# Moving the bias, v's copies and two statistics steps off GpSimd in a fused attention and FP4 feed-forward layer

## The reference

```python
xn = (x - mean) / sqrt(var + eps)
q, k, v = rope(xn @ Wqa @ Wqb), rope(k of xn @ Wkva @ Wkvb), v of the same
attn = softmax(causal(q @ k.T * scale)) @ v @ Wout + bout
h = silu(fp4(xn) @ fp4(w_gate).T) * (fp4(xn) @ fp4(w_up).T)
out = x + attn + fp4(h) @ fp4(w_down).T
```

## Time and profile before

| | |
|---|---|
| median of 3 runs | 807.89 us (806.34 to 809.37) |
| the profiled execution, its time and its span | 808.11 us, 806.0 us |
| PE busy in the span | 718.5 us (89%), 6354 instructions |
| DVE | 641.2 us (80%) |
| POOL | 612.4 us (76%) |
| ACT | 535.1 us (66%) |
| mean granted TensorE clock | 0.98 |

### The profile page before, as it was taken

How to read it: one execution, slowest core, us unless ns; L and a number is a source line. 1 busy time by engine, 2 the same in 40 slices (tenths; PEclk the granted TensorE clock), 3 DMA queues, 4 the chain that set the end, 5 groups by cost and what they waited for, 6 DMA issues and landing times.

```text
span 806.0 us, 18255 instructions
## 1 busy us (share of the span) xinstructions
PE 718.5 (89%) x6354; PEld 444.2 (55%) x6445; DVE 641.2 (80%) x1378; ACT 535.1 (66%) x1154; POOL 612.4 (76%) x708
## 2 busy tenths in 40 slices
PE   2366889999999999999999999999999999999773
PEld 1233555665656565656656565656566565656243
DVE  5569788989888988889898889888898988788110
ACT  2212677777686867777777868677777777575850
POOL 4534597878799797978787897979787888756560
PEclk9998899999999999999999999999999999999995
DMA  4423233243343334343434333343324333330111
GB/s 111 114 67 96 63 93 95 89 116 96 103 111 103 88 114 106 112 100 91 115 97 107 102 110 87 113 106 116 96 90 118 94 95 111 88 92 29 56 55 28
DMA packets 85589, 76.04 MB, mean 94 GB/s; under 512 B 28946, under 2 KB 67314, under 8 KB 85498
## 3 DMA queue, kind: packets, MB, share of 16 engines
q1 hardware_dynamic: 85498, 74.87, 34.3%
HBM read 40.73 MB, written 27.53 MB: 85 GB/s over the span
## 4 chain that ended last, share of the span: by engine, by line
PE 35%; POOL 32%; ACT 14%; issue 6%; DVE 6%; DMA 3%; SPq 2%; another core or an unknown queue 1%; POOLq 0%; DVEq 0%; ACTq 0%
POOL P L535 9%; PE pv_ps L1111 8%; PE exp_ps L1090 6%; POOL h L545 5%; ACT P L912 5%; PE max_ps L1075 5%; POOL h L548 5%; POOL h L551 4%; PE misc_ps L1135 3%; PE misc_ps L1143 3%; DVE neg_max L718 3%; PE max_ps L1076 3%; PE misc_ps L1160 3%; ACT h_mag L1019 3%; POOL q_split L626 2%
## 5 line engine op out<-in xcount | busy, mean ns | idle before, releaser
L718 DVE TENSOR_REDUCE neg_max<-max_ps 128x1 f32<-128x512 f32 (+3 forms) x768 | 429.1, 591 | 88.3 <-PE max_ps L1076 86.6
L912 ACT ACTIVATE P<-exp_ps 128x512 f32<-128x512 f32 x512 | 294.9, 599 | 167.0 <-remote 100.4
L1075 PE MATMUL max_ps<-K,Q 128*128 128x384 bf16 (+2 forms) x768 | 199.2, 278 | 23.4 <-DMA Kd<-K 11.2
L1090 PE MATMUL exp_ps<-Q,K 128*128 128x128 bf16 (+3 forms) x933 | 209.9, 293 | 10.8 <-ACT P L912 6.7
L1076 PE MATMUL max_ps<-Kd,Q 128*128 128x128 bf16 x1024 | 191.4, 221 | 1.4 <-DVE neg_max L718 1.3
L535 POOL TENSOR_SCALAR_AFFINE_SELECT P<-P 128x512 f32<-128x512 f32 x256 | 161.9, 667 | 26.8 <-ACT P L915 26.8
L1111 PE MATMUL pv_ps<-P,V 128*32 128x512 f32 (+3 forms) x2048 | 163.9, 438 | 1.9 <-POOL P L535 0.8
L1075 PEld LDWEIGHTS max_ps<-K,Q 128*128 128x128 bf16 x768 | 75.9, 100 | 92.1 <-DVE neg_max L718 47.1
L1076 PEld LDWEIGHTS max_ps<-Kd,Q 128*128 128x128 bf16 x1024 | 98.6, 100 | 45.6 <-issue 23.2
L1090 PEld LDWEIGHTS exp_ps<-Q,K 128*128 128x128 bf16 x1024 | 79.6, 98 | 48.6 <-ACT P L912 27.0
L566 POOL TENSOR_TENSOR h<-gate_sb,up_half 128x352 f32<-128x352 f32 x64 | 59.7, 932 | 56.8 <-DVE gate_sb L731 56.6
(11 more groups left out here) (109 smaller groups left out, 977.5 us busy)
## 6 DMA issues: line engine op xcount, KB each, us to landing
Q<-q_scr SPq DMA_DIRECT2D x64, 224.0 KB
o_scr<-oT SPq DMA_DIRECT2D x32, 256.0 KB, 2.5
q_scr<-q_split SPq DMA_DIRECT2D x16, 384.0 KB, 2.6
Kd<-K SPq DMA_DIRECT2D x64, 96.0 KB
x_in<-x SPq DMA_DIRECT2D x16, 256.0 KB, 4.6
q_scr<-q_split SPq DMA_DIRECT2D x16, 256.0 KB, 2.9
x_res<-x SPq DMA_DIRECT2D x16, 256.0 KB, 5.5
o_raw<-o_scr SPq DMA_DIRECT2D x32, 128.0 KB
```

The source lines that it names most:

```text
L718: nc.vector.tensor_reduce(neg_max[:, pr // 4, heads[0]:heads[0] + len(heads), pr % 4, i], max_ps[r % 3][:, 0:len(heads) * n].rearrange("p ...
L912: nc.scalar.activation(P[g % 2][:, hh + r % 2, col:col + 512], ps[:, :], ACT.Exp, scale=SCALE).then_inc(exp_done, 1)
L1075: nc.tensor.matmul(ps[:, col:col + d], Qt, Kt[:, half, g, 0:d], start=True, stop=True)
L1090: last = nc.tensor.matmul(exp_ps[n % 2][:, col:col + width], K[par][:, half, pr // 2, kb * 128:(kb + 1) * 128], Q[par][:, pr, kb * 128:S], ...
```

## The change

Four things are done. The bias bout becomes a 97th row of the third piece of wdT, beside a row of ones in hqT, so that PE's output matmul adds it; x_bias goes, DVE adds x_res itself, and SP loads x_res for batch T-1 in iteration T, behind the last read of "out1" of the iteration before. v_stage goes: DVE writes v from PSUM into V with two copies, and there are three V tiles in place of two. Of `statistics`, POOL keeps rstd alone; var_eps is made by DVE between two reductions of slot 3, and shift by DVE ahead of the first reduction of slot 5, behind a wait for rstd (neg_mean is folded into it). At the start DVE sets the row of ones, and POOL clears a third V tile.

```diff
+    def third(self, off):
+        return (self.t0 + off) % 3
-        V = [sb(f"V{i}", [128, NT, KVH, 32]) for i in range(2)]
+        V = [sb(f"V{i}", [128, NT, KVH, 32]) for i in range(3)]
...
 # SP
-                (bout_sb[:, :], bout.partition_broadcast(128)),
+                (wdT[FC[2][1]:FC[2][1] + 1, 2, :], bout.unsqueeze(0)),
...
-                if T.has(0):
-                    T.wait(sp, x_bias_done, 1, 0, 0)
-                    sp.dma_start(x_res[:, :, :], x[T.batch(0)]...).then_inc(x_res_loaded, 16)
+                if T.has(-1):
+                    T.prev().misc_wait(sp, misc_read, "out1")
+                    sp.dma_start(x_res[:, :, :], x[T.batch(-1)]...).then_inc(x_res_loaded, 16)
...
 # GpSimd
-            def statistics(T):
+            def deviation(T):
                 if not T.has(3):
                     return
-                T.wait(pool, mv_done, NT, 3, NT)
-                nc.gpsimd.tensor_scalar(var_eps[:, :], bn_mv[:, :, 1], EPS, None, ALU.add).then_inc(var_done, 1)
-                nc.gpsimd.tensor_scalar(neg_mean[:, :], bn_mv[:, :, 0], -1.0, None, ALU.mult).then_inc(var_done, 1)
-                T.wait(pool, var_done, 2, 3, 2)
+                T.wait(pool, var_done, 1, 3, 1)
                 nc.gpsimd.tensor_tensor(rstd[:, :], var_eps[:, :], half_neg[:, :], ALU.pow).then_inc(rstd_done, 1)
-                T.wait(pool, rstd_done, 2, 3, 1)
-                nc.gpsimd.tensor_tensor(shift[:, :], neg_mean[:, :], rstd[:, :], ALU.mult).then_inc(rstd_done, 1)
...
-                if T.has(1):
-                    T.prev().misc_wait(pool, misc_read, "v")
-                    if T.has(-1):
-                        T.wait(pool, pv_done, KVH, -1, KVH)
-                    for s in range(2):
-                        nc.gpsimd.tensor_copy(V[T.par(1)]..., v_stage...).then_inc(v_ready, 1)
...
-                if T.has(0):
-                    T.wait(pool, x_res_loaded, 16, 0, 16)
-                    T.misc_wait(pool, misc_read, "out1")
-                    nc.gpsimd.tensor_tensor(x_bias[:, :, :], x_res[:, :, :], bout_sb...).then_inc(x_bias_done, 1)
...
 # VectorE
-                                        x_bias[:, c, :], ALU.add).then_inc(misc_read[0], 1)
+                                        x_res[:, c, :], ALU.add).then_inc(misc_read[0], 1)
...
-                reduces(3, 4, 5)
+                reduces(3, 4)
+                if T.has(3):
+                    T.wait(dve, mv_done, NT, 3, NT)
+                    T.wait(dve, rstd_done, 2, 2, 1)
+                    nc.vector.tensor_scalar(var_eps[:, :], bn_mv[:, :, 1], EPS, None, ALU.add).then_inc(var_done, 1)
+                reduces(3, 5)
                 if T.has(2):
                     T.misc_wait(dve, misc_filled, "v")
-                    T.wait(dve, v_ready, 2, 1, 2)
-                    nc.vector.tensor_copy(v_stage[:, :, :], misc_ps[1][:, 0:128]...).then_inc(misc_read[1], 1)
+                    if T.has(-1):
+                        T.wait(dve, pv_done, KVH, -1, KVH)
+                    for odd in range(2):
+                        nc.vector.tensor_copy(V[T.third(2)][:, :, odd::2, D * odd:D * odd + D],
+                                              misc_ps[1][:, 0:128]...[:, :, odd::2, :]
+                                              ).then_inc(v_ready if odd == 0 else misc_read[1], 1)
...
+                if T.has(3):
+                    T.wait(dve, rstd_done, 2, 3, 1)
+                    nc.vector.scalar_tensor_tensor(shift[:, :], bn_mv[:, :, 0], -1.0, rstd[:, :],
+                                                   ALU.mult, ALU.mult).then_inc(rstd_done, 1)
                 reduces(5, 0)
                 normalize(T)
...
+            nc.vector.memset(hqT[FC[2][1]:FC[2][1] + 1, 2, :], 1.0).then_inc(ones_row, 1)
...
 # TensorE
-                        for k, (_, cn) in enumerate(FC):
+                        for k, cn in enumerate((FC[0][1], FC[1][1], FC[2][1] + 1)):
                             last = nc.tensor.matmul(ps[:, tok[n]], hqT[0:cn, k, tok[c]], wdT[0:cn, k, :], ...)
```

More of the change, by code:

```diff
@@ L151, in build @@
         wout_sb = sb("wout_sb", [E, E])
-        bout_sb = sb("bout_sb", [128, E])
         cosq_sb = sb("cosq_sb", [128, S])
@@ L171, in build @@
         rstd = sb("rstd", [128, NT])
-        neg_mean = sb("neg_mean", [128, NT])
         shift = sb("shift", [128, NT])
@@ L185, in build @@
         k_split = sb("k_split", [128, 3, 128], BF16)
-        v_stage = sb("v_stage", [128, NT, KVH * D])
         Q = [sb(f"Q{i}", [128, NPAIR, S], BF16) for i in range(2)]
@@ L203, in build @@
         x_res = sb("x_res", [128, NT, E])
-        x_bias = sb("x_bias", [128, NT, E])
         y = sb("y", [128, NT, E])
@@ L237, in build @@
         const_dma = sem("const_dma")
+        ones_row = sem("ones_row")
         factors_in = sem("factors_in")
@@ L280, in build @@
         x_res_loaded = sem("x_res_loaded")
-        x_bias_done = sem("x_bias_done")
         stored = sem("stored")
@@ L459, in iteration @@
             def iteration(T):
-                if T.has(0):
-                    T.wait(sp, x_bias_done, 1, 0, 0)
-                    sp.dma_start(x_res[:, :, :], x[T.batch(0)].rearrange("(c p) e -> p c e", p=128)).then_inc(x_res_loaded, 16)
+                if T.has(-1):
+                    T.prev().misc_wait(sp, misc_read, "out1")
+                    sp.dma_start(x_res[:, :, :], x[T.batch(-1)].rearrange("(c p) e -> p c e", p=128)).then_inc(x_res_loaded, 16)
                 scatter_sums(T, -1, 1)
@@ L515, in _ @@
             nc.gpsimd.memset(half_neg[:, :], -0.5).then_inc(consts_set, 1)
-            for i in range(2):
+            for i in range(3):
                 nc.gpsimd.memset(V[i][:, :, :, :], 0.0).then_inc(pool_const, 1)
@@ L520, in _ @@
             nc.gpsimd.memset(m_split[:, :, 64:128], 0.0).then_inc(pool_const, 1)
-            pool.wait_ge(pool_const, 5)
-            for i in range(2):
+            pool.wait_ge(pool_const, 6)
+            for i in range(3):
                 nc.gpsimd.memset(V[i][:, :, 0::2, 2 * D:2 * D + 1], 1.0).then_inc(pool_const, 1)
@@ L603, in iteration @@
                     causal(T, 0, 0)
-                if T.has(1):
-                    T.prev().misc_wait(pool, misc_read, "v")
-                    if T.has(-1):
-                        T.wait(pool, pv_done, KVH, -1, KVH)
-                    for s in range(2):
-                        nc.gpsimd.tensor_copy(V[T.par(1)][:, :, s::2, D * s:D * s + D],
-                                              v_stage[:, :, :].rearrange("p c (g d) -> p c g d", g=KVH)[:, :, s::2, :]).then_inc(v_ready, 1)
                 if T.has(2):
@@ L633, in iteration @@
                     nc.gpsimd.tensor_tensor(k_split[:, 2, :], k_rest[:, :], k_split[:, 1, :], ALU.subtract).then_inc(k_pool, 1)
-                statistics(T)
+                deviation(T)
                 split_rest(T, 1, 0)
@@ L644, in iteration @@
                     quantize(T, 0, 3, *hs)
-                if T.has(0):
-                    T.wait(pool, x_res_loaded, 16, 0, 16)
-                    T.misc_wait(pool, misc_read, "out1")
-                    nc.gpsimd.tensor_tensor(x_bias[:, :, :], x_res[:, :, :],
-                                            bout_sb[:, :].unsqueeze(1).to_broadcast([128, NT, E]), ALU.add).then_inc(x_bias_done, 1)
                 if T.has(3):
@@ L765, in output @@
                 if n == 0:
-                    T.wait(dve, x_bias_done, 1, -1, 1)
+                    T.wait(dve, x_res_loaded, 16, -1, 16)
                     T.wait(dve, stored, 32, -1, 0)
@@ L831, in iteration @@
                     T.wait(dve, x_loaded, 16, 3, 16)
-                    T.wait(dve, var_done, 2, 2, 2)
                     for c in range(NT):
@@ L843, in iteration @@
                         nc.vector.bn_aggr(bn_mv[:, c, :], bn_raw[:, c, :]).then_inc(mv_done, 1)
-                reduces(3, 4, 5)
+                reduces(3, 4)
[4 more added lines that the diff above has]
+                reduces(3, 5)
                 if T.has(2):
                     T.misc_wait(dve, misc_filled, "v")
-                    T.wait(dve, v_ready, 2, 1, 2)
-                    nc.vector.tensor_copy(v_stage[:, :, :], misc_ps[1][:, 0:128].rearrange("p (c n) -> p c n", c=NT)).then_inc(misc_read[1], 1)
+                    if T.has(-1):
+                        T.wait(dve, pv_done, KVH, -1, KVH)
+                    for odd in range(2):
+                        nc.vector.tensor_copy(V[T.third(2)][:, :, odd::2, D * odd:D * odd + D],
+                                              misc_ps[1][:, 0:128].rearrange("p (c g d) -> p c g d", c=NT, g=KVH)[:, :, odd::2, :]
+                                              ).then_inc(v_ready if odd == 0 else misc_read[1], 1)
                 reduces(4, 0)
@@ L1042, in _ @@
             pe.wait_ge(proj_ready, 1)
-            pe.wait_ge(pool_const, 11)
+            pe.wait_ge(ones_row, 1)
+            pe.wait_ge(pool_const, 14)
             def transpose_weights():
@@ L1104, in weighted_sums @@
```

(5 more changed lines are left out.)

## The result

The changed kernel takes 836.68 us (median of 4 runs, 832.57 to 842.28), the kernel before 808.02 beside it: a ratio of 1.036, 95% interval 1.0295 to 1.0426. The forecast of 827 had the sign and the place right and the size wrong: 29 us more in place of 19, and outside its range. The profiled execution takes 835.48, its span is 833.4 against 806.0, and its mean granted clock 0.961 against 0.980.

What follows compares the result with a forecast made beforehand. PE was taken to bound the kernel, POOL close behind. From 808.1 us, twelve iterations at +1.70 (+2.12 - 0.42) add 20.4 and T = 0 takes off 0.9: 827 us, range 800 to 833.

Steps and rivals of the forecast that it cites:

- Bias, copies, x_res: Bias row, v's copies and the x_res load: nothing taken as gain, with up to 0.6 us of DVE as other end.
- the idle time ahead of slot 4: DVE's 0.60 us of waiting for PE before slot 4's first reduction, said to cover at most 0.50 us of added work.
- POOL is ahead and onT falls behind the long step: In slot 5, POOL's long step on h starts before onT is asked for, so PE's output product comes 2.1 us later.
- +1.70 us per iteration: Net loss in T = 1 to 12: +2.12 at PE's output product, less 0.42 at hqT0, to 46.06 us.
- +2.1: Delay of PE's first output product, 425.12 against 423.00, with onT behind POOL's long step on h; +1.9 if shift doesn't wait.
- the 0.42 gained back: From output product to hqT0, 10.16 us in place of 10.58, since PE no longer waits for POOL there.
- holding the long step up by 0.24: DVE's shift waits for POOL's fourth h product, so POOL's long step starts at 421.57 in place of 421.33.
- 0.93 us ahead: POOL's lead behind k_split without var_eps, neg_mean and shift: long step on h at 421.33 in place of 422.26.
- DVE is later still: Rival: shift waits for POOL's first long step on h, onT for the second; +54 us, 861 in all; chance 0.13.
- 4.5 forecast: Cost per iteration if DVE is later still: +4.9 us at PE's output product, less 0.4.
- forecast -0.9: T = 0 has no onT; of its 1.51 us wait at hqT0, POOL's 0.93 goes.

Runs made afterwards that it cites:

- statistics back on POOL: Changed kernel with all four statistics steps back on POOL, the bias row, v's copies and x_res staying changed: 805.02 us, 0.9969 of the kernel before.
- POOL made to wait: Changed kernel with one more wait, so POOL begins its first long step on h only when onT is made: 803.96 us, ratio 0.9961 to the kernel before.
- the swap: Kernel of shift on POOL with onT put ahead of slot 5's first reduction on DVE: 808.48 us, ratio 1.0024 to the kernel before.
- shift on POOL: Changed kernel with shift back on POOL behind rstd, var_eps and neg_mean on DVE: 838.50 us, ratio 1.0382 to the kernel before.
- the last run: Changed kernel with only onT and slot 5's first reduction swapped on DVE, no wait on POOL: 843.01 us, ratio 1.0450 to the kernel before.
- twelve products: Changed kernel with twelve throwaway products on PE ahead of its wait for onT: 839.04 us, ratio 1.0399 to the kernel before.
- seven products: Changed kernel with seven throwaway products on PE ahead of its wait for onT: 828.26 us, ratio 1.0268 to the kernel before.
- statistics alone: Kernel before with only var_eps and shift moved to DVE: 834.17 us, ratio 1.0342 to the kernel before.

## Why the forecast was right in its place and wrong in its size

**Bias, copies, x_res: right.** Together they are worth 0.3% (statistics back on POOL), where the forecast had put them at nothing. var_eps (0.17) and two copies (0.22 each) fit under the idle time ahead of slot 4, which is 0.53 us now.

**POOL is ahead and onT falls behind the long step: right**, shown by undoing it three ways: statistics back, POOL made to wait, and the swap. The rule cited in the forecast (the Trainium skill, SBUF — State Buffer, "Who interferes with whom"), that the one that is issued first holds the ports for its whole instruction, agrees with the pair of shift on POOL, where onT started 0.05 us behind the long step and waited for all of it, and, the other way round, with T = 2 of the same kernel swapped, where the long step started behind onT and took 3.31 us in place of 2.85. The two pairs of the last run neither bear it out nor refute it: by the profile DVE starts 0.02 us ahead in both, and onT got through in one.

**The sum's "+1.70 us per iteration" is the step that failed, by a term that it lacks.** Without a fall of the clock it is 45.58 - 44.36 = +1.2: hqT0 to the output product 35.41 against 33.78, +1.6 where I had +2.1, and from there 10.16 against 10.58, the 0.42 gained back as forecast. The +2.1 was too large by 0.5. Half of it is shift, which I had holding the long step up by 0.24: it takes 0.34 us with its own wait, but the long step begins right behind the fourth product (197.68 + 0.92 against 198.56). The other half is POOL, which I had 0.93 us ahead: the long step begins 31.86 us behind hqT0 in T = 2, against 33.05 in T = 7 of the kernel before, so 1.19 ahead. What failed is that I took PE's idle time at its own length. In seven of the twelve iterations it also took the clock down, for another 1.6 us each, and in T = 5 the clock fell as well. T = 13 of the kernel before, with 1.24 us of idle time, had shown the wait without the fall, and I carried that over to a wait of 2. The windows behind that wait, in the kernel before:

```profile
689.93:694.00 4.07, 4.07 (x42) 3.05 (x44) 3.17 (x7) 0.60 (x1) 3.47 (x3) 1.00 0.40 103
```

Keeping PE busy through the wait removed every iteration of 47.2, with twelve products and with seven. The Trainium skill (TensorE: Matmul & The Clock Gate, "HAM oscillation — how this bites in real kernels") describes such a loop, in which a wait in each round throttles PE again. The trace agrees in part: the clock fell behind the wait in 7 rounds of 12, and the waits, of 1.96 us, are shorter than those of the page's kernel.

**The rival "DVE is later still" isn't a case for the whole run, as I had it, but one for single iterations**: one of twelve here, two with seven products, by a DMA that landed late, and one in statistics alone. In T = 5 it cost 6.5 us, the clock included, against 4.5 forecast.

By the span: 4 x 1.2 + 7 x 2.8 + 6.5 = 30.9, and -2.1 up to hqT0 of T = 0 (forecast -0.9), -0.1 in T = 13 to 15, -1.6 behind the last hqT0: 27.1 of the 27.4 measured. Behind the last hqT0 the mean clock is 0.82 against 0.69 in the kernel before; what raised it, and what shortened the start, I did not trace further. That the forecast is only 10 us off (8 by the profiled execution) is in part luck: the fall of the clock (7 x 1.6) and T = 5 (5.3 above the others) added 16.5 us that it lacked, and the 0.5 too much in the +2.1 (12 x 0.5), the start and the end took back 9.

**Left open**: why the clock falls behind some waits of 1.96 us and not behind others. Its length alone doesn't decide: in the changed kernel with onT swapped a stall of 3.11 us (T = 4) left the clock at 1.00.

## What to carry to other kernels

When work leaves GpSimd, lay its new timeline beside VectorE's and look at which of their instructions now come first where both read tiles in SBUF: here 0.6 us of order between two instructions decided nearly 4%. An instruction that PE waits for should hold that order by a wait or by its place in the list, not by luck: one wait on POOL and one swap on DVE turned 836.7 us into 800. And a stall of PE isn't priced by its length alone: look at what the granted clock does behind it, for stalls of that length, not of shorter ones.

## What the runs showed of the hardware

- A 128x4 step on DVE can wait for as long as a large one, with one tile to read (var_eps) as with two (shift): var_eps 0.16 to 1.12 us, shift 0.15 to 2.11 us in the changed kernel (2.57 in statistics alone), by what POOL has just begun.
- The order is decided within a few hundredths of a us: onT, started 0.05 us behind POOL's long step, lost its turn; started 0.02 us ahead by the profile, it went either way.
- Behind 1.95 to 1.97 us of idle time PE's clock fell to 0.50 in 14 of 22 iterations (the changed kernel and statistics alone), behind 2.21 to 2.23 us in 9 of 11 and behind 1.64 us in one of one (shift on POOL). Behind 1.24 and 1.28 us in the kernel before (T = 13 and 14) it stayed at 1.00.
